# The order of key tiles within a query block of two causal attentions

## The reference, cut to what matters

```python
# first attention: 16 heads of 32, 8 key-value heads
att = jnp.einsum('bhqd,bhkd->bhqk', q, k) * scale
att = SOFTCAP * jnp.tanh(att / SOFTCAP)
att = jnp.where(causal, att, -jnp.inf)
y = jnp.einsum('bhqk,bhkd->bhqd', softmax(att), v)
# third stage: 16 heads of 16, 4 key-value heads, no cap
```

## Time and profile before

| what | us |
|---|---|
| median of 3 runs | 2923.03 |
| lowest and highest | 2917.98, 2935.89 |
| the profiled execution | 2921.05 |
| its span, from first to last instruction | 2919.3 |
| first attention `aa` (exp first and last start) | 118.5 to 422.3 |
| plain attention `ab` (exp first and last start) | 664.6 to 996.9 |

### The profile page before, as it was taken

How to read it: one execution, slowest core, us unless ns; L and a number is a source line. 1 busy time by engine, 2 the same in 40 slices (tenths; PEclk the granted TensorE clock), 3 DMA queues, 4 the chain that set the end, 5 groups by cost and what they waited for, 6 DMA issues and landing times. The chain is left out here.

```text
span 2919.3 us, 68814 instructions
## 1 busy us (share of the span) xinstructions
PE 2475.7 (85%) x25231; PEld 1672.4 (57%) x25320; DVE 1966.3 (67%) x4308; ACT 1710.6 (59%) x3452; POOL 850.7 (29%) x1233
## 2 busy tenths in 40 slices
PE   8888878888888788888888888869998887899998
PEld 4433336643333375545555555557887566788988
DVE  6488886667787467698788889863333255576652
ACT  2598875324445453388788888843222334676778
POOL 2244432111101122355555555510000222232223
PEclk9999889978999899899999999989999677899999
DMA  5533302244333112602220322013000568522210
GB/s 181 147 80 79 79 0 78 86 109 60 51 37 45 37 52 104 140 8 30 30 32 2 38 23 30 2 39 141 1 1 21 89 153 173 69 30 32 37 41 8
DMA packets 280880, 175.04 MB, mean 60 GB/s; under 512 B 204769, under 2 KB 241137, under 8 KB 278513
## 3 DMA queue, kind: packets, MB, share of 16 engines
q1 hardware_dynamic: 271392, 162.45, 26.6%
q10 hardware_dynamic: 9168, 8.41, 1.2%
HBM read 111.75 MB, written 54.66 MB: 57 GB/s over the span
## 5 line engine op out<-in xcount | busy, mean ns | idle before, releaser
L1463 ACT ACTIVATE ad_e<-ps,ad_nm 128x1024 f32<-128x1024 f32 (+7 forms) x512 | 380.1, 744 | 110.7 <-DVE ad_nm L1548 104.9
L1548 DVE TENSOR_REDUCE ad_nm<-ps 128x1 f32<-128x1024 f32 (+7 forms) x512 | 372.3, 752 | 40.7 <-PE ps L1396 31.5
L706 ACT ACTIVATE ab_e<-ps 128x512 f32<-128x512 f32 (+3 forms) x384 | 167.0, 490 | 193.8 <-PE ps L621 192.6
L1394 PE MATMUL ps<-fd_k_st,fd_q_st 96*128 96x512 bf16 (+3 forms) x768 | 215.9, 341 | 54.3 <-ACT ad_e L1463 49.1
L1577 DVE CUSTOM_DVE_ANT_0 ad_t<-ad_e,ad_rz 128x128 f32<-128x128 f32 (+7 forms) x256 | 208.1, 813 | 42.2 <-POOL ad_e L1513 23.1
L1513 POOL TENSOR_SCALAR ad_e<-ad_e,ad_c 128x128 f32<-128x128 f32 (+7 forms) x256 | 191.9, 750 | 19.7 <-DVE ad_c L1565 17.8
L1409 PE MATMUL ps<-ident,ad_t 128*128 128x128 f32 x1152 | 171.6, 277 | 26.3 <-ACT ad_prT L1473 13.1
L1989 POOL TENSOR_TENSOR st_it_low<-st_it,st_it_high 128x256 fp32r<-128x256 f32 x128 | 98.8, 783 | 320.9 <-ACT st_it_high L2252 314.8
L1473 ACT ACTIVATE ad_prT<-ps 128x128 f32<-128x128 f32 (+7 forms) x256 | 166.2, 649 | 21.2 <-PE ps L1417 21.1
L1504 POOL TENSOR_SCALAR_AFFINE_SELECT ad_e<-ad_e 128x128 f32<-128x128 f32 x256 | 90.8, 354 | 297.6 <-ACT ad_e L1463 272.4
L711 ACT ACTIVATE aa_e<-ps 128x1024 f32<-128x1024 f32 (+1 forms) x192 | 150.1, 828 | 37.0 <-PE ps L621 33.5
(11 more groups left out here) (383 smaller groups left out, 7098.6 us busy)
## 6 DMA issues: line engine op xcount, KB each, us to landing
scr_a<-pa_parts SPq DMA_DIRECT2D x24, 512.0 KB, 2.8
fa_q_st<-scr_a SPq DMA_DIRECT2D x24, 512.0 KB, 7.9
split<-f_split SPq DMA_DIRECT2D x16, 768.0 KB, 3.9
fd_q_st<-scr_d SPq DMA_DIRECT2D x48, 256.0 KB, 7.8
g_w<-split SPq DMA_DIRECT2D x8, 1536.0 KB, 18.2
scr_d<-pd_parts SPq DMA_DIRECT2D x20, 384.0 KB, 2.6
st_w_first<-split ACTq DMA_DIRECT2D x5, 1536.0 KB, 8.2
fa_k_st<-scr_a SPq DMA_DIRECT2D x24, 256.0 KB, 8.6
```

Source lines behind the costliest of these rows:

```text
L706: act.activation(e[:, u % ER, h, lo:QB], m.ps[:, n4(u, h) % 3, lo:QB], ACT.Exp, scale=scale).then_inc(s_read[0], 1)
L1394: last = pe.matmul(m.ps[:, bank, 0:n], q_st[:, b, 2 * h + s, t * P:(t + 1) * P], k_st[:, b, s, cc * QB:cc * QB + n], start=True, stop=True)
L1463: act.activation(e[:, u % EB, s, 0:L], src, ACT.Exp, bias=nm[:, u % EB, s:s + 1], accum_out=z[:, u % EB, s:s + 1]).then_inc(exped[s], 1)
L1548: dve.tensor_reduce(nm[:, u % EB, s:s + 1], src, AX.X, ALU.max, negate=True).then_inc(maxed[s], 1)
```

## The change: tiles from both ends in turn

The list of steps takes the key tiles of a query block from the front and from the back in turn. Block 0 becomes `kt` 0, 3, 1, 2, with widths 4, 1, 3, 2; block 1 becomes `kt` 0, 7, 1, 6, 2, 5, 3, 4, with widths 4, 1, 4, 2, 4, 3, 4, 4. The lags, the order within a slot, all sizes and counts of instructions stay. A block still ends at steps 3 and 11 (now `kt` 2 and `kt` 4, both diagonal), and still starts with `kt` 0. The masks keep their number, eight a group, four a block; in block 1 they come at steps 5, 7, 9 and 11 instead of 8 to 11. The waits on `masked` count masks by a table. Both attentions share the list, so both change.

```diff
-    steps = [(qb, kt) for qb in range(T // QB) for kt in range((qb + 1) * QB // P)]
+    steps = []
+    for qb in range(T // QB):
+        tiles = range((qb + 1) * QB // P)
+        steps += [(qb, tiles[n // 2] if n % 2 == 0 else tiles[-1 - n // 2]) for n in tiles]
     NS, NQ = len(steps), T // QB
     PER, ITERS = 2 * NS, B * GB // 2
-    ends = {s: qb for s, (qb, kt) in enumerate(steps) if kt == (qb + 1) * QB // P - 1}
+    ends = {s: qb for s, (qb, kt) in enumerate(steps) if s + 1 == len(steps) or steps[s + 1][0] != qb}
+    masks_to = [sum(kt * P >= qb * QB for qb, kt in steps[:s + 1]) for s in range(len(steps))]
...
-                    wait(pe, masked, i, 2 * BT, g * BT + kt + 1)
+                    wait(pe, masked, i, 2 * BT, g * BT + masks_to[s])
...
-                    wait(dve, masked, i, 2 * BT, g * BT + kt + 1)
+                    wait(dve, masked, i, 2 * BT, g * BT + masks_to[s])
```

## The result

| | before | changed |
|---|---|---|
| median of 20 runs, us | 2931.71 | 2938.26 |
| lowest and highest | 2915.91, 2940.56 | 2929.77, 2947.22 |
| profiled execution | 2921.05 | 2937.94 |
| its span | 2919.3 | 2936.2 |
| mean granted TensorE clock | 0.917 | 0.907 |

The changed kernel takes 1.0028 times as long (95% interval 1.0016 to 1.0040), some 8 us more; the two medians lie 6.6 us apart. That is small, but on the side opposite to the forecast and outside its range. The trace of before was taken from an execution near the low end of its runs, so the two traces, 16.9 us apart, show the loss about twice as large as it is over all runs. The forecast started from that execution too. Counted from the median of the twenty runs it would be 2919, with a range up to 2937.7, and 2938.26 still lies just outside.

What follows compares the result with a forecast made beforehand. ACT and DVE, nearly full, were taken to bound the first attention, PE and DVE the plain one. From the profiled 2921.05 us, less 16.8 and plus 4 gave 2908.3, forecast as 2908, range 2898 to 2917 (chance 0.50).

Steps and rivals of the forecast that it cites:

- What bounds the stage: First attention: ACT and DVE nearly full; ACT's 36.0 us of waits before widest and narrowest tanh were the ceiling.
- the sum's 19.2: First attention: new waits before the tanh of steps 3 and 7, 2.4 us a group, 19.2 in all.
- chain A: End of block 1: exp, mask, accumulation, denominators, scores, 7.3 us against ACT's 6.0; 1.2 us wait before step 3.
- chain B: End of block 0, through mask, DVE, denominators and scores: 10.0 us against ACT's 8.8; 1.2 us wait before step 7.
- then a pair of scores: Last term of the chain at block 1's end: one pair of scores on PE, estimated at about 0.5 us.
- I take 16.8, since evener widths give PE fewer thin stretches: First attention: 36.0 us of waits gone less 19.2 new, without PE's half clock, which would leave 2.4.
- Rival 2: First attention: new block ends, with half clock on denominators, replace the old waits; 2923 us, no change; chance 0.22.
- Rival 3: DVE, first attention: accumulations sit out masks, 1.27 us each; eight a group give 2950 us, six 2929; chance 0.10.
- Rival 1: First attention: the even order works in full, no chain late, all 36 us gained; 2889 us; chance 0.18.
- forecast at +4: Plain attention: 2.9 us on the row maxima's chain in slot 1, 1.3 for a wide last step; ends -7 and +10.
- slots that became lighter were taken as worth nothing: Plain attention, slot 10: 1.05 us less PE work, counted as no gain because DVE is late there.

Runs made afterwards that it cites:

- the filler: Changed kernel plus two unread 128x512 matmuls in ten of twelve slots of the first attention; 0.9915 of the kernel before, exps of the stage 297.5 us.
- filler and select: Changed kernel with those unread matmuls and POOL masking by affine select instead of the multiply by keep; 0.9873 of the kernel before, exps 284.9 us.
- alone-run: Kernel before with the new order in the plain attention alone; 0.9982 of the kernel before (0.9962 to 1.0002).
- the narrow end: Front and middle tiles in turn, blocks ending on their narrowest step, with unread matmuls and affine select; 0.9847 of the kernel before, 2886.3 us.

## Why the prediction was wrong

**What bounds the stage: right.** ACT and DVE were near full, and the new order removed the waits before the narrowest tanh, 23.9 to 1.5 us. POOL had a large share in them: the affine select alone, in the old order, took them to 9.4, and 18 us off DVE's accumulations with them.

**What is late next: right places, one term at nothing.** Both chains showed before the tanh of steps 3 and 7. At full clock the waits there are 28.6 us, against the sum's 19.2. The chains themselves were sized well, even a little too long: the waits before the first tanh of these slots are 15.4 us in all, mostly 0.8 to 0.9 at chain A and 1.2 to 1.3 at chain B, for 1.2 each (chain A's own terms, 7.3 less 6.0, make 1.3). What the sum left out is "then a pair of scores": a slot has two pairs, and the second stands behind the weighting. That term was put at nothing and measures 0.83 us at nearly every one of these slots, 13.2 in all.

**The step that failed** is "I take 16.8, since evener widths give PE fewer thin stretches". It was the other way round. As ACT no longer waited, it ran full for more than a slot with 2.54 us in 4 for PE beside it, and the granted clock fell to the 1.2 GHz level at both ends of blocks. In the kernel before it did so in some groups only. All waits of the stage were 55.4 us, where the sum had 19.2, and the clock alone is worth 24.9 us of the stage in this order, as the filler shows.

**Rival 2 was the right one and still too small.** It had the half clock, but charged it to the denominators alone (0.9 a chain, 33.6 us of waits). At that place everything of PE takes nearly twice as long, two weightings (1.93 and 1.94 for 1.07) and the scores as well. Measured: 55.4.

**Rival 3 fell.** L831's total is 131.0, its undisturbed sum, with DVE busy 253 us in the stage: no accumulation sat out a mask in the new order. In the prediction the lock's price went to DVE's sums; what was left of it in the new order fell on POOL (two masks in 3.63 us beside a wide sum) and on DVE's copies. The same copy takes 1.23 us alone and 2.29 beside a mask (232.79 in the timeline). With the filler, the 16 copies take 30.5 us in all, where they took 19.6 in the kernel before. So engines can hold each other up elsewhere than at semaphores.

**Rival 1** would have needed both remedies. Even with filler and select the changed order keeps 20.2 us of waits.

**The plain attention** was forecast at +4 and lies between -5 and 0. It stayed within the bounds of -7 to +10, but its likely sign was wrong. The interval of its alone-run, 0.9982, includes no change, so the step (slots that became lighter were taken as worth nothing) is doubtful rather than refuted.

## What to carry to other kernels

When two engines are brought into balance, ask what the third does meanwhile. TensorE beside a well-fed ACT can lose its clock, and the price comes due at the next burst of matmuls, on all of them. The granted clock of the few microseconds around a stall tells this, where PE's busy share does not; a filler of matmuls that nobody reads is a cheap test.

An even order has to be judged by what a block ends on. Taken by itself, with clock and mask mended, the order of this change is worth next to nothing in the stage (284.9 against 285.5 us), and the other even order, which ends narrow, is worth 9 (276.2). These are single traces; in runs of the whole program the narrow end was 7.3 us ahead of the changed order (2886.3 against 2893.6, four runs each, which do not overlap).

A lock between two engines must be priced on both. And a chain through an engine that works strictly in order ends at the last thing its reader needs, here the second pair of scores, with all that stands in the queue before it.

## What the runs showed that I had not expected

Useless matmuls in the queue of an engine that is already busy some 80% of the stage made both kernels faster, by 0.85% and 0.63% of the program against the kernel before. And the affine select not only takes less time than the multiply by `keep` but also leaves DVE's sums nearly alone: in the kernel before, with that one edit, L827's total (L828 there) is 133.3 us, where it was 151.5:

```profile
114.00:432.00 318.00, 133.29 (x80) 0.93 0.31 66
```

Its own 64 executions still average 1.27 us in that kernel (81.3 us in all), twice the 0.64 of the plain attention, so it still waits for DVE's sums there. The rows show this one-sidedness:

```profile
183.49 2.29 DVE L828 TENSOR_TENSOR aa_e_sum<-aa_e_sum,aa_e 128x2048 f32<-128x2048 f32 x1
183.63 2.65 POOL L763 TENSOR_SCALAR_AFFINE_SELECT aa_e<-aa_e 128x512 f32<-128x512 f32 x1 [0.17 <-ACT aa_e L718]
```
